# Weight look-up in a four-layer transformer kernel: a second set of leaf buffers, and table functions and choices at other heads

## The reference

```python
x = x + _L2_xattn_ref(_layernorm(x), ctx_1024, ...)   # 16 heads of width 16, 256 queries x 256 keys, softmax
x = x + _L2_ffn_ref(_layernorm(x), lut, gate_idx, up_idx, down_idx)

def _ghost_linear(x, idx, lut):      # lut: 16 floats, idx: int32 from 0 to 15
    w = lut[idx]
    return jnp.einsum('bsh,oh->bso', x, w)
```

## Time and profile before

| | |
|---|---|
| Time, median of 3 runs | 938.35 us (933.8 to 938.6) |
| Profiled execution, its own time | 932.58 us |
| Its span, first to last instruction | 930.8 us |
| TensorE busy | 851.7 us (92%) |
| VectorE busy | 652.0 us (70%) |
| ScalarE busy | 529.2 us (57%) |
| GpSimd busy | 389.1 us (42%) |
| Mean granted clock of TensorE | 0.972 |

### The profile page before, as it was taken

The page is one execution under the profiler, slowest core; times in us unless marked ns, Lnnn a source line. Parts: engine busy times, 40 slices in busy tenths (PEclk is TensorE's granted clock), DMA queues, the critical chain, the costliest instruction groups (busy, mean ns, idle before and its releaser), DMA issues.

```text
span 930.8 us, 13235 instructions
## 1 busy us (share of the span) xinstructions
PE 851.7 (92%) x4430; PEld 611.3 (66%) x4430; DVE 652.0 (70%) x1242; ACT 529.2 (57%) x1011; POOL 389.1 (42%) x334
## 2 busy tenths in 40 slices
PE   5888999999999999976897999998998889999998
PEld 3566878777878778743543854787987754454746
DVE  6569899989898988787775357667777656443211
ACT  3487778777877787984334455545677663112110
POOL 2136777878787778647557325011000003400000
PEclk9999999999999999997999999999999889999999
DMA  5022000000000000110120201000000004000000
GB/s 172 18 77 93 18 18 17 17 17 17 17 17 17 17 20 1 52 46 1 45 69 7 86 1 34 1 1 1 1 1 1 1 1 144 1 0 1 22 1 23
DMA packets 12587, 25.44 MB, mean 27 GB/s; under 512 B 4296, under 2 KB 8032, under 8 KB 11200
## 3 DMA queue, kind: packets, MB, share of 16 engines
q1 hardware_dynamic: 10288, 21.59, 7.2%
q10 hardware_dynamic: 2256, 3.28, 1.0%
HBM read 23.82 MB, written 1.05 MB: 27 GB/s over the span
## 4 chain that ended last, share of the span: by engine, by line
PE 36%; DVE 12%; ACT 5%; POOL 3%; issue 3%; DVEq 0%; ACTq 0%; POOLq 0%
PE PS L2630 14%; PE PS L2644 7%; PE PS L2814 3%; DVE max_groups L2028 2%; PE PS L2599 1%; DVE stats L1364 1%; PE PS L2417 1%; PE PS L2157 1%; ACT regA L1309 1%; PE PS L2443 1%; ACT regC L1289 1%; PE PS L2582 1%; POOL regA L690 1%; POOL regA L685 1%; PE PS L2798 1%
## 5 line engine op out<-in xcount | busy, mean ns | idle before, releaser
L612 POOL TENSOR_TENSOR X<-X,xn 128x512 f32<-128x512 f32 x62 | 106.8, 1722 | 62.1 <-ACT xn L902 61.1
L571 POOL TENSOR_SCALAR veps<-mv 128x4 f32<-128x4 f32 (+1 forms) x20 | 5.9, 296 | 283.8 <-DVE mv L1369 281.8
L2814 PE MATMUL PS<-regA 128*128 128x128 f32 x512 | 74.9, 294 | 9.3 <-ACT regA L1309 9.3
L926 ACT ACTIVATE regA<-PS,nb,rq 128x256 f32<-128x256 f32 x128 | 72.2, 577 | 11.9 <-DVE regA L1470 11.1
L1493 DVE TENSOR_TENSOR_SCAN regB<-regB 128x1024 f32<-128x1024 f32 x30 | 78.6, 2620 | 0.5 <-POOL regA L690 0.3
L605 POOL TENSOR_TENSOR y<-y,regB 128x1024 f32<-128x1024 f32 x32 | 75.6, 2364 | 5.8 <-DVE regB L1504 5.7
L2814 PEld LDWEIGHTS PS<-regA 128*128 128x128 f32 x512 | 68.2, 207 | 13.2 <-ACT regA L1309 11.9
L2248 PE MATMUL PS<-regA 128*128 128x256 f32 x256 | 66.2, 380 | 4.5 <-DVE qss L1457 4.5
L2226 PE MATMUL PS<-regA 128*128 128x256 f32 x256 | 67.3, 386 | 2.4 <-ACT regA L876 2.2
L1470 DVE TENSOR_SCALAR_CACHE_REDUCE regA<-PS,nrq 128x256 bf16<-128x256 f32 x128 | 56.0, 475 | 19.1 <-PE PS L2226 17.2
L2257 PE MATMUL PS<-regA 128*128 128x256 f32 x256 | 65.7, 379 | 0.0
(11 more groups left out here) (337 smaller groups left out, 2014.1 us busy)
## 6 DMA issues: line engine op xcount, KB each, us to landing
regA<-in_W SPq DMA_DIRECT2D x16, 384.0 KB, 3.1
regB<-in_wg SPq DMA_DIRECT2D x2, 1024.0 KB, 6.5
regB<-in_wu SPq DMA_DIRECT2D x2, 1024.0 KB, 8.2
X<-in_x SPq DMA_DIRECT2D x2, 512.0 KB, 5.2
regC<-in_wg ACTq DMA_DIRECT2D x1, 1024.0 KB, 5.2
regC<-in_wu ACTq DMA_DIRECT2D x1, 1024.0 KB, 8.5
regC<-in_wd ACTq DMA_DIRECT2D x1, 1024.0 KB, 10.5
regB<-in_wd SPq DMA_DIRECT2D x1, 1024.0 KB, 4.8
```

The costliest lines, as they stand in the source:

```text
L612: pool.tensor_tensor(xt, xt, part, ALU.add).then_inc(x0_add, 1)
L926: act.activation(p0[i][:, q, :], bank(S_BANK + i)[:, q * S:(q + 1) * S], ACT.Exp, bias=nb0[:, i, q:q + 1], scale=rq[par][:, 2 * b + q:2 * ...
L2814: last = pe.matmul(bank(6 + g % 2)[:, at:at + P], pT2[i % 3][:, k, q * P:(q + 1) * P], V2flat[:, v:v + P], start=k == 0, stop=k == 1)
```

## The change

There is a second set of the four leaf buffers, used by the odd pieces. It takes room in `regB` (which overlaps the lowest bit and the first mask of late piece 0), in `regC` and in `q_low`. The steps are dealt out anew: ScalarE's leaves are at steps 1, 2, 4 and 5 (with nothing at step 3), VectorE has the bits at step 0, choices at steps 2, 3 and 5 and at steps 0 and 1 of the next piece (one, two, one, two, final). Leaves 0 and 1 of a piece wait for the choices of the piece two before, where they waited for all or nearly all of the piece before. `LUT_HEADS` gains head 39. `late_bits(0)` moves from head 61 to behind the last head.

```diff
+        lut_sets = [(*lut_alt, lutC, lutD),
+                    (regB[:, 10872:10872 + LP], regB[:, 10872 + LP:10872 + 2 * LP], regC[:, 3072:3072 + LP],
+                     q_low.rearrange("p t h d -> p (t h d)")[:, 0:LP])]
...
-        LUT_HEADS = [i for i in range(STEPS2) if i != 13 and (i >= 3 * H2 or i % H2 not in range(2 + (i >= H2), 13) or i in range(2 * H2 + 8, 2 * H2 + 13))]
+        LUT_HEADS = [i for i in range(STEPS2) if i != 13 and (i >= 3 * H2 or i % H2 not in range(2 + (i >= H2), 13) or i in range(2 * H2 + 7, 2 * H2 + 13))]
...
                 act.wait_ge(lut_bits, i + 1)
-                used = 7 * i + (0, 0, 1, 3)[k]
-                if used:
+                used = (7 * i - 7, 7 * i - 7, 7 * i + 1, 7 * i + 3)[k]
+                if used > 0:
                     act.wait_ge(lut_pick, used)
-                to = (w2[:, i * LP:(i + 1) * LP], lutC, lutD, lutC)[k]
-                for dst, leaf in ((to, 2 * k), (lut_alt[k % 2], 2 * k + 1)):
+                alt0, alt1, C, D = lut_sets[i % 2]
+                to = (w2[:, i * LP:(i + 1) * LP], C, D, C)[k]
+                for dst, leaf in ((to, 2 * k), ((alt0, alt1)[k % 2], 2 * k + 1)):
...
-                    if piece < LUT_LOOP and 1 <= step < 5:
-                        lut_leaves(piece, step - 1)
+                    if piece < LUT_LOOP and step not in (0, 3):
+                        lut_leaves(piece, (1, 2, 4, 5).index(step))
...
-                    if 0 < piece <= LUT_LOOP and step == 0:
-                        lut_step(piece - 1, 6)
-                    if piece < LUT_LOOP:
-                        lut_step(piece, step)
-                    if i == STEPS2 - 3:
-                        late_bits(0)
+                    if 0 < piece <= LUT_LOOP and step < 2 and i in LUT_HEADS:
+                        lut_step(piece - 1, step + 5)
+                    if piece < LUT_LOOP and step in (0, 2, 3, 5):
+                        lut_step(piece, min(step, 4))
...
+            late_bits(0)
             normalise(B - 1, H2 // HPB - 1)
             late_bits(1)
```

More of the change, by code:

```diff
@@ L2077, in lut_step @@
                     dve.wait_ge(lut_leaf, 4 * i + k + 1)
-                    choose((A, lutC, lutD, lutC)[k], m1, lut_alt[k % 2])
+                    choose((A, C, D, C)[k], m1, (alt0, alt1)[k % 2])
                     if k % 2:
                         dve.wait_ge(lut_pick, n + (2, 5)[k // 2])
-                        choose((A, lutD)[k // 2], m2, lutC)
+                        choose((A, D)[k // 2], m2, C)
                 elif step == 6:
                     dve.wait_ge(lut_pick, n + 6)
-                    choose(A, m3, lutD)
+                    choose(A, m3, D)
             for h in range(H2):
```

## The result

The changed kernel takes 939.14 us (median of 20 runs, 936.14 to 944.97), the kernel before beside it 935.99 us (median of 20 runs, 932.46 to 941.75). The ratio is 1.0039, 95% interval 1.0022 to 1.0056 (the quotient of the two medians is 1.0034): slower by 2.1 to 5.2 us, with the middle at 3.65. The forecast was +2.9 us, and 941 us as a time, which was reckoned from the 938.35 us of three runs; over 20 runs the kernel before takes 2.4 us less than that. The profiled execution of the changed kernel has a span of 936.7 us, against 930.8.

The account below looks back on a forecast made before the run. TensorE was taken to be held by waits for ScalarE's exponentials and VectorE's maxima, and by the clock falling after them. +1.4 + 0 - 3.5 + 3.0 + 2.0 = +2.9 us on 938.35 gave 941 us, range 934 to 946.

Parts of the forecast that it names:

- A: Starts of batch elements 1 and 2: later L3 delays the maxima, TensorE waits 0.7 us longer each, +1.4 us.
- The rival that the clock falls there: Longer waits at the starts of batch elements 1 and 2 pull the clock down: +6.7 us, 945; chance 0.25.
- B: Heads 39 to 46: a wait moves to the maxima, about 2.5 us there; 0, between -1 and +1.
- C: Heads 40 to 57: leaf pairs two and two lose less, -3 us, with the clock's -0.5 together -3.5.
- D: Heads 57 to feed-forward: layer norm 10 starts later and late bits come last; +3.0 us, ends +1.5 and +4.
- E: Feed-forward start: after TensorE stands still, matmuls run at half clock; +2.0 us, ends 0 and +3.
- The rival by which the time would fall: Four TensorE waits in heads 47 to 61, 6.55 us, all vanish: -5.2 us, 933; chance 0.15.
- the point that was to decide it: Near the end: whether layer norm 10 finds its place without holding L3 of piece 5 decides the faster rival.
- Nothing moves: Whole kernel: the same VectorE work sets the pace, costs at start and tail matching the middle's gain; 938, chance 0.15.

Follow-up runs that it names:

- e4: Changed kernel with pieces 0 and 1 put back on their old steps, pieces 2 to 5 as changed; 938.16 us, 1.0028 of before.
- e10: Order of before for pieces 2 to 5, one buffer set, late bits at head 61, new steps for pieces 0 and 1 alone; 937.39 us, 1.0013 of before.
- e1: Changed kernel with one set of leaf buffers instead of two, order untouched; 937.73 us, 1.0027 of before.
- e5: Kernel before with only the bits of late piece 0 moved from head 61 to behind the last head; 941.28 us, 1.0058 of before.
- e6: Kernel before with only layer norm 10 split, statistics at head 52 and application at head 58; 931.10 us, 0.9961 of before.
- e2: Changed kernel with one set of leaf buffers and the late bits back at head 61; 934.07 us, 0.9985 of before.
- e3: Changed kernel with layer norm 10 split, statistics at head 48 and application at head 54; 935.80 us, 1.0010 of before.
- e8: Changed kernel with one buffer set, late bits at head 61, layer norm 10 split at heads 48 and 54; 927.84 us, 0.9922; run again 930.57 us, 0.9939.
- e9: Changed kernel with 26 filler matmuls on TensorE ahead of the feed-forward's wait for the choices; 937.54 us, 1.0028 of before.

## Why the prediction was right, step by step

The sum was +2.9 us and the middle of the measured ratio is +3.65, interval 2.1 to 5.2. By its parts:

- **A, the starts.** Forecast +1.4; the traces of all kernels that have the new steps for pieces 0 and 1 show +1.2 to +1.4 (51.2 to 51.4 us against 50.0 to 50.2), with the waits forecast at 1.3 to 1.9 measured at 1.43 to 1.45. The rival that the clock falls there is refuted for the profiled executions: the clock is 1.00 in both windows above, and e4 and e10 show no loss of 4 us in the medians.
- **B, the maxima.** Forecast a wait of about 2.5 us in place of 0.97, measured 2.36, against the 1.96 us that vanished at the next head's values (0.63 are left of it in e1). From head 40 to head 47, 18.1 us became 17.3 to 17.4 in every trace of the new order: -0.8 where 0 was forecast, within its ends. This is part of the 40-57 stretch, and so of the numbers under C.
- **C, heads 40 to 57.** Forecast -3 without the clock. Measured, with B in it and with the one slow stretch near head 47 on both sides, 37.77 became 35.5 to 36.0, so -1.8 to -2.2; against the traces of the new order that have no slow stretch at all (34.8) it is -3.0, which has some of the clock in it. So without the clock C was forecast too large by about 1 us. With the clock the profiled pair gives -4.9 (40.80 to 35.92), where I had taken -3.5. The slow stretches of before near 729 us came in two of four traces of that order (before and e10, not e5 and e6), a share of a half where I took a sixth; they cost 3.0 us up to head 57 as I had them, but only 1.56 behind the layer norm, so that here one wrong size stood against the other.
- **D, to the feed-forward.** Forecast +3.0, measured 20.93 - 18.06 = +2.87. That the number agrees so well is luck, in two ways. The working of the prediction gives less than its sum: the layer norm later by 1.5 to 2 us and 11.4 us behind it against 11.25 are +1.7 to +2.2, not +3.0. And 18.06 belongs to an execution with the slow stretch near 729; without it before would take about 19.5 (estimated above), and D would be +1.4. In the profiled pair the layer norm starts 4.52 us after head 57's exponential and not 2.23, and the feed-forward 16.41 us after the layer norm's start and not 15.83: +2.3 and +0.6. The causes named were right: undoing the late bits alone takes 2.3 us off (e2 against e1), splitting the norm alone 3.2 (e3), both 6.8 (e8), more than the two together, since one delay was partly covered by the other. From head 40 to the feed-forward, where C and D are taken together and this split falls out, the forecast was -0.5 and the profiled pair gives -2.0 (58.86 to 56.85).
- **E, the clock at the feed-forward.** Forecast +2.0, ends 0 and +3. Measured 28.33 - 26.86 = +1.5 in the changed kernel, 3.1 in e1, 3.0 in e3, 1.7 in e4, 2.8 in e5, so 1.5 to 3.1 in all five without a filler that have the late bits at the end, and nothing in the nine other traces, which have them at head 61 or fill the wait. Against the mean of the five, 2.4, I was 0.4 short.

The rival by which the time would fall, that the second set closes the repeating gaps, failed on its first step: with one set all waits are the same (e1). And on the point that was to decide it, layer norm 10 did hold L3 of piece 5, for 3.10 us. The rule of the Trainium skill that the prediction weighed ("Perfetto Trace Analysis", section "Identifying Performance Opportunities") says that repeating gaps can mean too few buffers; the traces of this case don't agree that they do here (waits of 3.1, 2.9 and 1.9 us with one set, 3.1, 2.9 and 2.0 with two), because VectorE issues its choices ahead of the bits for which the next leaf waits anyway.

The parts can't be added from single traces, since before's has the slow stretch that only half of them have. An estimate from the rows: +1.3 (A), -1.75 (B, C and D together, head 40 to the feed-forward: the mean of 56.85, 55.69 and 56.47 in the changed kernel, e1 and e4, less 58.1, half way between 58.87 and 57.3), and +2.4 (E), together about +2.0 us, just below the interval of 2.1 to 5.2. So the forecast of +2.9 came near the 3.65 with the waits and their causes right, and with sizes of single parts off by up to some 1.5 us that stood against each other. "Nothing moves" was wrong by its parts, which are each several microseconds but for A, and its sum of nothing lies outside the interval. What stays open is the split of the 3.65 us by medians, and the 1.7 us between it and the estimate: A alone is beneath what these executions can tell.

## What to carry to other kernels

Where two engines pass work to and fro, look first at whether a wait ends on a buffer or on a value; a second buffer set helps only with the first, and here it forbade the one placement (the late bits in the loop) that hid work. Follow a reordering to the end of the loop: the gain of the middle, 2 to 5 us by the clock of the execution, was lost at the tail, where the last piece met a long instruction group (the layer norm) and a step that had to move. Splitting that group into VectorE's own waits gave 0.9961 by itself, and together with the new order and one set 0.992 to 0.994, faster than both kernels. And price a stretch of the trace from one execution with care: the same order of steps took 40.8 us or 37.8 from head 40 to 57, by where the clock fell, and half of the difference was taken up by the next wait.

## What the runs showed of the hardware

In the five traces in which TensorE stood still for 2.6 to 5.2 us ahead of the feed-forward (2.61 in e4, 3.19 in e5, 3.53 in the changed kernel, 3.54 in e1, 5.19 in e3), matmuls at 1.2 GHz (a granted clock of 0.50) followed, at a cost of 1.5 to 3.1 us. In the eight with one of 1.3 to 1.6 us there, and in e9 with none, they did not. The two of 1.45 and 1.43 us at the starts left it at 2.4 GHz (1.00 in both windows). The length of the wait alone doesn't settle it: a wait of 2.36 us near head 47 was followed by 3.4 us at 0.50 in the changed kernel, and the same wait, 2.37 us, by none in e1. An f32 matmul is two records in these traces, not one: 26 in e9 are 52 records of 0.11 us each, and the eight records of a head's values are four matmuls, while the eight f32 transposes of a layer norm are eight records.
